# Four attentions in one kernel: the second score tile of a step is issued and read behind the step's piece instead of beside the first tile

## The chip, the cores and the metric

The kernel runs on one core of a Trainium2 chip. The metric is the device time of the whole program in microseconds (us); lower is better. The core's engines run side by side and meet only through semaphores: PE (the matrix engine, TensorE), DVE (VectorE), ACT (ScalarE), POOL (GpSimd) and SP, whose queue issues the DMAs.

## The reference

Four transformer layers on `x` of shape 4 x 512 x 256, each an attention of 16 heads of 16 dims and a feed-forward part, both with a layer norm in front and a residual sum behind:

```
x = x + _L0_attn_ref(_layernorm(x), ...)   # distances, window mask of 64, 8 key heads
x = x + _L0_ffn_ref(...)
x = x + _L1_attn_ref(_layernorm(x), ...)   # causal
x = x + _L1_ffn_ref(...)
x = x + _L2_attn_ref(_layernorm(x), ...)   # causal, rotary
x = x + _L2_ffn_ref(...)
x = x + _L3_attn_ref(_layernorm(x), ...)   # no mask
x = x + _L3_ffn_ref(...)
...
attn = softmax(q @ k.T * scale + mask)     # per head, 512 x 512
out  = attn @ v
```

## The kernel before

The first attention (called a0 here) is `attention_window`, the other three (a1, a2, a3) are `attention_quads`; a1 and a2 are causal, a3 has no mask. The change touches the loop of these two functions and nothing else.

**Two kinds of scores.** The softmax is taken over keys, and the kernel wants the exponentials with keys on the partitions, so that they can be multiplied with V without a transpose. So it computes the scores twice. First `scores(t)` makes a tile with 128 queries on the partitions (up to 512 keys in the columns, fewer in the causal attentions), and DVE reads it only for the row maxima: `maxima(t)` (`minima(t)` in a0), L1165 and L440. Below such a tile is called s. When the 16 tiles of a group of four heads are read, POOL splits the maxima into two numbers (`split_maxima`), PE turns them, and ACT and DVE write them into rows of q, so that the second product has the maximum subtracted. Then `scores_T(N)` makes the transposed scores of two heads (two matmuls, called T below), ACT takes their exponential, and `values(J)` multiplies two steps' exponentials with V (called V).

**Two halves of the array.** A head's q and k take 64 partitions: head a = 0 the partitions 0 to 63, head a = 1 the partitions 64 to 127. Matmuls of T and s therefore use 64 of PE's 128 rows ("64*128" in the profile's rows), those of V and of the pieces use all. s tiles alternate: tile 2N + 24 has a = 0 and PSUM bank 4, tile 2N + 25 has a = 1 and bank 5. Below s0 and s1 are these two tiles of step N. A tile may be written only when the tile before it in its bank is read (`pe.wait_ge(max_done, t - 1)`).

**Steps and pieces.** A batch and attention has 32 steps, there are four batches, so 128 steps N per attention. The s tiles run 24 tiles (LEAD) ahead of T. A table `plan` puts at most one piece into each step: all the rest of the attention cut up, each piece using PSUM bank 7: `turn` and `project` make the next batch's q and k, `values` its V, `maxima` the turn of the maxima, `group` the turn of a finished group (DVE then divides, `finish_group`), `heads` and `outputs` the output product. Before it writes bank 7, PE waits until the piece before is taken out of it (`freed`).

PE's program order in a step is T, s0, s1, V (in odd steps), piece. DVE's is maxima of s0, maxima of s1, its share of the piece, then an `exchange` (rotary) or layer norm work of a later batch in a few steps. ACT's is the exponential and its share of the piece. In the causal attentions every s and T is followed by two short matmuls that add the mask in the same half and bank (L1423, L1425 and L1447, L1451); in a0 T is (L708).

Of the kernel before, what the change touches and what calls it, by code (L numbers as in the profile page):

```python
# [14 lines left out]
NB = 4  # L15
# [144 lines left out]
def attention_window(nc, tag, X, cst, PS, scr, filled, weights, rope, scale, dist, slopes, masks, preset_m, bias):  # L160
# [8 lines left out]
    TILES_ = 2 * STEPS  # L169
    LEAD = 24  # L170
# [5 lines left out]
    with ExitStack() as ctx:  # L176
# [101 lines left out]
        with nc.Block() as block:  # L278
# [137 lines left out]
            def _(dve):  # L416
# [99 lines left out]
                sigmoid(1)  # L516
                keep_minima(0, 0)
                for N in range(FULL):
                    for t in (2 * N + LEAD, 2 * N + LEAD + 1):
                        if t < NB * TILES_:  # L520
                            minima(t)
                    piece(*piece_at(N))
                    if N % STEPS in swaps and N // STEPS + 1 < NB:
                        exchange(N // STEPS + 1, swaps[N % STEPS])
                    c = N // STEPS + 2
                    if c < NB:
                        if N % STEPS == 23:
                            layer_norm_stats(dve, ln, c, source(c))
                        elif N % STEPS == 25:
                            dve.wait_ge(transposed, 2 * KC * c)  # L530
                            layer_norm_apply(dve, ln, c, source(c))
                        elif N % STEPS == 26:
                            total(c)
                        elif N % STEPS == 28:
                            sigmoid(c)
                for x in LAST:
                    piece(*x)

# [102 lines left out]
            def _(pe):  # L641
# [155 lines left out]
                pe.wait_ge(masks_done, 2)  # L797
                for N in range(FULL):
                    scores_T(N)
                    for t in (2 * N + LEAD, 2 * N + LEAD + 1):  # L800
                        if t < NB * TILES_:
                            scores(t)
                    if N % 2 and N >= 3:
                        values((N - 3) // 2)
                    piece(*piece_at(N), previous_piece(N))
                values(FULL // 2 - 1)
                before = previous_piece(FULL)
                for x in LAST:
# [6 lines left out]
def attention_quads(nc, tag, X, Y, cst, PS, scr, filled, weights, spans, masks=None, rope=None, bias=None,  # L815
# [13 lines left out]
    LEAD = 24  # L829
    FULL = NB * STEPS  # L830
    SCALE = HD ** -0.5
    with ExitStack() as ctx:
# [319 lines left out]
        def vector_program(dve):  # L1152
            p = Names()

            def source(c):
                return lambda t: X[:, TB * c + t, :]
# [91 lines left out]

            def loop():
                for N in range(FULL):  # L1250
                    for t in (2 * N + LEAD, 2 * N + LEAD + 1):
                        if t < NB * TILES_:
                            maxima(t)
                    piece(*piece_at(N))
                    if N % STEPS in swaps and N // STEPS + 1 < NB:
                        exchange(N // STEPS + 1, swaps[N % STEPS])
                    if N % STEPS == 24 and N // STEPS + 2 < NB:
                        layer_norm_stats(dve, ln, N // STEPS + 2, source(N // STEPS + 2))
                    if N % STEPS == 26 and N // STEPS + 2 < NB:
                        dve.wait_ge(transposed, KC * (N // STEPS + 2))  # L1260
                        layer_norm_apply(dve, ln, N // STEPS + 2, source(N // STEPS + 2))
                for last in LAST:
                    piece(*last)

# [112 lines left out]
        def tensor_program(pe):  # L1377
# [164 lines left out]
            def loop():  # L1542
                for N in range(FULL):
                    scores_T(N)
                    for t in (2 * N + LEAD, 2 * N + LEAD + 1):
                        if t < NB * TILES_:
                            scores(t)
                    if N % 2 and N >= 3:
                        values((N - 3) // 2)
                    piece(*piece_at(N), previous_piece(N))  # L1550
                values(FULL // 2 - 1)
                before = previous_piece(FULL)
                for last in LAST:
# [1777 lines left out]
```

## Time and profile before

| | |
|---|---|
| device time, median of 3 runs | 1834.86 us (1834.26 to 1839.75) |
| the profiled execution's own time | 1827.52 us |
| its span, first to last instruction | 1825.7 us |
| busy share of the span | PE 88%, PE's weight loads 53%, DVE 62%, ACT 48%, POOL 26% |
| loops of the attentions, from the span's start | a0 about 70 to 336 us, a1 532 to 767, a2 914 to 1148, a3 1420 to 1673 |

The profile is one execution. It rests on the start and end of every instruction; for PE the ends are modelled, so a busy PE is not a PE at its peak, and two matmuls in different halves of the array count as one busy stretch. Weight loads (PEld) are rows of their own. In a row of a timeline the first number is the start in us from the span's start, the second the length in us, and the bracket behind it tells how long the engine sat idle before it and what ended that.

### The profile page before, as it was taken

To read this page: it belongs to the slowest core of one execution; us is meant where nothing else is said; L and a number is where in the kernel's file an instruction comes from. 1 tells how busy PE (TensorE), PEld (TensorE's weight loads), DVE (VectorE), ACT (ScalarE), POOL (GpSimd) and SP (SyncE) were. 2 spreads that over 40 slices of the span, in tenths; PEclk is the share of its full clock that TensorE was granted. 3 is DMA by queue.
4 is the path that set the end of the run, shared out by engine and by line. 5 is a ranking of instruction groups with operands and counts; after the bars stand their busy time and mean duration, and the time that the engine had idled before them with its cause. 6 is when DMAs were issued, how large, how long until landed. Compare 5 with 4: busy or idle time off the path is not lost. (4 is left out here: it accounts for less than half of the span.)

```text
span 1825.7 us, 28978 instructions
## 1 busy us (share of the span) xinstructions
PE 1608.8 (88%) x10726; PEld 963.0 (53%) x10726; DVE 1134.3 (62%) x2567; ACT 867.9 (48%) x1361; POOL 469.0 (26%) x596
## 2 busy tenths in 40 slices
PE   5899999799989999952999999689999999998776
PEld 2344444388866666541556665367764444443533
DVE  2787787333446666468577776355545788774475
ACT  1256565533325555532155555457761666665322
POOL 4222210033322330010333220036762522300000
PEclk9999999999989999965999999879999999999698
DMA  7452350200235424000643560211206435320322
GB/s 248 107 128 65 81 145 1 95 0 0 77 91 162 133 80 114 1 10 27 178 116 83 128 162 2 87 45 54 80 25 174 112 80 145 115 48 13 112 94 93
DMA packets 68962, 160.30 MB, mean 88 GB/s; under 512 B 10286, under 2 KB 15927, under 8 KB 67963
## 3 DMA queue, kind: packets, MB, share of 16 engines
q1 hardware_dynamic: 68826, 158.51, 30.6%
q8 instruction: 83, 1.36, 0.3%
q14 instruction: 53, 0.43, 0.1%
HBM read 109.05 MB, written 53.09 MB: 89 GB/s over the span
## 5 line engine op out<-in xcount | busy, mean ns | idle before, releaser
L1165 DVE TENSOR_REDUCE a_mx<-PS 128x1 f32<-128x512 f32 (+3 forms) x768 | 392.3, 551 | 188.1 <-PE PS L1425 128.1
L1362 ACT ACTIVATE a_pT<-PS 128x1024 f32<-128x1024 f32 (+3 forms) x384 | 310.2, 811 | 228.1 <-PE PS L1451 159.2
L1420 PE MATMUL PS<-a_k,a_q 64*128 64x512 f32 (+3 forms) x768 | 233.9, 415 | 16.7 <-DVE a_mx L1165 13.6
L440 DVE CUSTOM_DVE_ANT_0 PS<-PS,a_dist 128x448 f32<-128x448 f32 x256 | 156.1, 643 | 51.1 <-PE PS L685 48.7
L1442 PE MATMUL PS<-a_q,a_k 64*128 64x512 f32 (+3 forms) x768 | 174.0, 437 | 7.2 <-PEq L98 2.0
L1465 PE MATMUL PS<-a_pT,a_va 128*32 128x512 f32 (+3 forms) x1536 | 164.5, 500 | 3.1 <-ACT a_raw L1315 2.9
L590 ACT ACTIVATE a_pT<-PS 128x448 f32<-128x448 f32 (+1 forms) x256 | 124.6, 541 | 84.6 <-PE PS L708 84.2
L1442 PEld LDWEIGHTS PS<-a_q,a_k 64*128 64x128 f32 x768 | 76.0, 185 | 144.9 <-issue 70.5
L1420 PEld LDWEIGHTS PS<-a_k,a_q 64*128 64x128 f32 x768 | 109.0, 187 | 69.9 <-DVE a_mx L1165 57.0
L157 PE MATMUL PS<-cst 128*128 128x512 f32 x192 | 102.9, 667 | 36.7 <-PEq L98 28.6
L2361 POOL TENSOR_TENSOR f_h_low<-f_prod,f_h_high 128x512 fp32r<-128x512 f32 x84 | 109.9, 1315 | 60.4 <-ACT f_h_high L2548 57.6
L1423 PE MATMUL PS<-a_half_masks 64*128 64x128 bf16 x512 | 100.6, 229 | 0.0
L2484 DVE TENSOR_TENSOR f_prod<-PS,f_gb 128x512 f32<-128x512 f32 x84 | 57.3, 688 | 67.8 <-ACT PS L2574 65.9
L685 PE MATMUL PS<-a_k,a_q 64*128 64x448 f32 x256 | 86.1, 461 | 12.1 <-DVE a_mx L440 5.5
L1290 ACT ACTIVATE a_q<-PS 16x1024 fp32r<-16x1024 f32 x48 | 48.7, 1014 | 79.2 <-PE PS L1473 78.8
L1425 PE MATMUL PS<-a_half_masks 64*128 64x64 bf16 x512 | 86.3, 190 | 0.0
L2574 ACT ACTIVATE PS<-PS,f_b 128x512 f32<-128x512 f32 x84 | 55.4, 660 | 50.2 <-PE PS L2648 50.0
L157 PEld LDWEIGHTS PS<-cst 128*128 128x128 f32 x192 | 36.2, 207 | 75.7 <-issue 68.4
L1102 POOL TENSOR_TENSOR a_mxh<-a_mx,a_m 128x16 fp32r<-128x16 f32 x48 | 10.8, 225 | 239.2 <-DVE a_mx L1165 239.2
L721 PE MATMUL PS<-a_pT,a_va 128*32 128x512 f32 x512 | 68.2, 604 | 1.6 <-ACT a_raw L598 1.1
L1710 POOL TENSOR_TENSOR f_h_low<-f_hid,f_h_high 128x512 fp32r<-128x512 f32 x32 | 41.2, 1292 | 94.3 <-ACT f_h_high L1809 94.3
L1170 DVE TENSOR_SCALAR a_q<-PS 16x1024 fp32r<-16x1024 f32 x48 | 59.0, 1230 | 7.3 <-PE PS L1473 5.7
(362 smaller groups left out, 3436.6 us busy)
## 6 DMA issues: line engine op xcount, KB each, us to landing
spread_scratch<-a_high SPq DMA_DIRECT2D x96, 256.0 KB, 3.0
a_q<-spread_scratch SPq DMA_DIRECT2D x96, 256.0 KB, 5.5
a_k<-spread_scratch SPq DMA_DIRECT2D x96, 256.0 KB, 6.2
f_gb<-gate_rows SPq DMA_DIRECT2D x68, 256.0 KB, 5.2
spread_scratch<-a_low SPq DMA_DIRECT2D x48, 256.0 KB, 4.0
a_q<-window_scratch SPq DMA_DIRECT2D x32, 256.0 KB, 5.6
a_k<-window_scratch SPq DMA_DIRECT2D x32, 256.0 KB, 6.4
window_scratch<-a_high SPq DMA_DIRECT2D x24, 256.0 KB, 4.7
```

Of the source, the lines that this page charges most:

```text
L157: pe.matmul(PS[:, bank, :], cst[:, C_ID:C_ID + P], cst[:, 0:512], start=True, stop=True)
L440: dve.tensor_tensor_reduce(PS[:, 4 + a, 0:KW], PS[:, 4 + a, 0:KW], dt_[:, off:off + KW], 1.0, 3e38, ALU.add, ALU.min, mx[:, gg % 2, qt, 2 ...
L590: act.activation(pT[rows, buffer_of(kt), 2 * half + a, GLOB:S], PS[rows, 2 * half + a, GLOB:S], ACT.Exp, scale=-float(slopes[2 * pair + a] ...
L685: pe.matmul(PS[:, 4 + a, 0:KW], q[rows, b % 2, pair, qt * P:(qt + 1) * P], k[rows, b % 2, pair, GLOB:S], start=True, stop=True).then_inc(s ...
L1165: dve.tensor_reduce(mx[:, gg % 2, qt, 2 * half + a:2 * half + a + 1], PS[:, tile_bank(t), 0:kw], AX.X, ALU.max).then_inc(max_done, 1)
L1362: act.activation(pT[:, N // 2 % 2, N % 2, :, q0:S], PS[:, 2 * (N % 2):2 * (N % 2) + 2, q0:S], ACT.Exp, scale=SCALE).then_inc(exp_done, 1)
L1420: mm = pe.matmul(ps[:, 0:kw], q[b % 2][rows, pair, qt * P:(qt + 1) * P], k[b % 2][rows, pair, 0:kw], start=True, stop=not causal)
L1423: pe.matmul(ps[:, kw - P:kw], half_masks[rows, 0, 0, :], half_masks[rows, 1, 0, :], start=False, stop=False)
L1425: mm = pe.matmul(ps[:, kw - 64:kw], half_masks[rows, 0, 1, :], half_masks[rows, 1, 1, 64:P], start=False, stop=True)
L1442: mm = pe.matmul(PS[:, 2 * half + a, q0:S], k[b % 2][rows, pair, kt * P:(kt + 1) * P], q[b % 2][rows, pair, q0:S], start=True, stop=not ca ...
L1465: mm = pe.matmul(PS[BLK * i:BLK * i + BLK, 6, q0:S], va[b % 2][:, kt, GH * g + i, :], pT[:, J % 2, i // 2, i % 2, q0:S], start=(kt == 0), ...
L2361: pool.tensor_tensor(h_low[:, G % 6, :], prod[:, G % 6, :], h_high[:, G % 6, :].bitcast(F32), ALU.subtract).then_inc(h_low_done, 1)
```

## The change

In all four attentions the second s tile of each step moves to the step's end. On PE the order becomes T, s0, V (in odd steps), piece, s1. On DVE it becomes maxima of s0, exchange or layer norm work, the piece, maxima of s1. No instruction is added, removed or resized; ACT, POOL and SP keep their order. The tiles' banks and waits stay: s1 still waits for the maxima of the s1 before.

```diff
@@ DVE, attention_quads (attention_window alike)
                 for N in range(FULL):
-                    for t in (2 * N + LEAD, 2 * N + LEAD + 1):
-                        if t < NB * TILES_:
-                            maxima(t)
-                    piece(*piece_at(N))
+                    if 2 * N + LEAD < NB * TILES_:
+                        maxima(2 * N + LEAD)
                     if N % STEPS in swaps and N // STEPS + 1 < NB:
                         exchange(N // STEPS + 1, swaps[N % STEPS])
...
                         layer_norm_apply(dve, ln, N // STEPS + 2, source(N // STEPS + 2))
+                    piece(*piece_at(N))
+                    if 2 * N + LEAD + 1 < NB * TILES_:
+                        maxima(2 * N + LEAD + 1)
@@ PE, both functions
                     scores_T(N)
-                    for t in (2 * N + LEAD, 2 * N + LEAD + 1):
-                        if t < NB * TILES_:
-                            scores(t)
+                    if 2 * N + LEAD < NB * TILES_:
+                        scores(2 * N + LEAD)
                     if N % 2 and N >= 3:
                         values((N - 3) // 2)
                     piece(*piece_at(N), previous_piece(N))
+                    if 2 * N + LEAD + 1 < NB * TILES_:
+                        scores(2 * N + LEAD + 1)
```

PE in a3, a stretch of three steps (from 1506.59 us of the trace). L1442 are the two T, L1420 the s tiles, L1479 the piece that turns a finished group, L1465 V, L1473 the piece that turns the maxima. Before:

```order
L1442 MATMUL PS<-a_q_17470,a_k_17471 128x512 x2
L1420 MATMUL PS<-a_k_17471,a_q_17470 128x512 x2
L1479 MATMUL PS<-cst,a_raw 128x128 x4
L1442 MATMUL PS<-a_q_17470,a_k_17471 128x512 x2
L1420 MATMUL PS<-a_k_17471,a_q_17470 128x512 x2
L1465 MATMUL PS<-a_pT,a_va_17476 32x512 x4
L1442 MATMUL PS<-a_q_17470,a_k_17471 128x512 x2
L1420 MATMUL PS<-a_k_17471,a_q_17470 128x512 x2
L1473 MATMUL PS<-cst,a_m 128x128 x4
```

The same steps after the change (T is now L1445, s L1423, V L1468, the pieces L1482 and L1476):

```order
L1445 MATMUL PS<-a_q_17470,a_k_17471 128x512 x2
L1423 MATMUL PS<-a_k_17471,a_q_17470 128x512
L1482 MATMUL PS<-cst,a_raw 128x128 x4
L1423 MATMUL PS<-a_k_17471,a_q_17470 128x512
L1445 MATMUL PS<-a_q_17470,a_k_17471 128x512 x2
L1423 MATMUL PS<-a_k_17471,a_q_17470 128x512
L1468 MATMUL PS<-a_pT,a_va_17476 32x512 x4
L1423 MATMUL PS<-a_k_17471,a_q_17470 128x512
L1445 MATMUL PS<-a_q_17470,a_k_17471 128x512 x2
L1423 MATMUL PS<-a_k_17471,a_q_17470 128x512
L1476 MATMUL PS<-cst,a_m 128x128 x4
```

Each T now stands between two single s tiles: s1 of the step before, in the upper half, ahead of it, and its own s0, in the lower half, behind it.

DVE in a1, the place in the second batch where layer norm statistics of a later batch (L126 to L130) meet the piece `outputs` (L1204, after the change L1206). Before:

```order
L1204 TENSOR_TENSOR X<-X,PS 128x512
L126 BN_STATS a_ln_stats<-X 128x6 x4
L128 MEMSET a_ln_held 128x1
L130 BN_AGGR a_ln_meanvar<-a_ln_stats 128x2 x4
L1165 TENSOR_REDUCE a_mx<-PS 128x1 x4
```

After:

```order
L126 BN_STATS a_ln_stats<-X 128x6 x4
L128 MEMSET a_ln_held 128x1
L130 BN_AGGR a_ln_meanvar<-a_ln_stats 128x2 x4
L1206 TENSOR_TENSOR X<-X,PS 128x512
L1167 TENSOR_REDUCE a_mx<-PS 128x1 x4
```

The piece's read of bank 7 now stands behind the statistics; the place is there once in a1 and once in a2.

## Rows read from the trace of the kernel before

**Rows 1.** The page: span, and busy us, share of the span, instructions by engine.

```profile
span 1825.7 us, 28978 instructions
PE 1608.8 (88%) x10726; PEld 963.0 (53%) x10726; DVE 1134.3 (62%) x2567; ACT 867.9 (48%) x1361; POOL 469.0 (26%) x596
```

**Rows 2.** Windows over the loops of a0 and a3: length, each engine's busy us, PE's clock, DMA.

```profile
80.00:345.00 265.00, 252.61 (x1752) 116.45 (x1751) 196.81 (x570) 159.32 (x311) 47.22 (x83) 1.00 0.29 75
...
1420.00:1680.00 260.00, 249.26 (x1381) 112.30 (x1380) 191.10 (x319) 168.41 (x191) 60.74 (x90) 1.00 0.32 86
```

**Rows 3.** Waits, whole span: who waited for whom, us in total, times, longest.

```profile
PEld PS L1420 <- DVE a_mx L1165: 57.0, 120, 1.8
PEld PS L685 <- DVE a_mx L440: 34.3, 82, 1.1
```

**Rows 4.** Timeline of a3, PE, its weight loads and DVE, 1504.9 to 1509.2.

```profile
1504.93 0.51 PE L1442 MATMUL PS<-a_q,a_k 64*128 64x512 f32 x2
...
1505.59 1.07 PE L1465 MATMUL PS<-a_pT,a_va 128*32 128x512 f32 x8
...
1506.59 0.49 PE L1442 MATMUL PS<-a_q,a_k 64*128 64x512 f32 x2
1506.92 0.61 PE L1420 MATMUL PS<-a_k,a_q 64*128 64x512 f32 x2
1507.04 0.18 PEld L1420 LDWEIGHTS PS<-a_k,a_q 64*128 64x128 f32 x1 [0.15 <-DVE a_mx L1165]
...
1507.42 1.29 DVE L1165 TENSOR_REDUCE a_mx<-PS 128x1 f32<-128x512 f32 x2 [0.44 <-PE PS L1420]
...
1507.46 0.65 PE L1479 MATMUL PS<-cst,a_raw 128*128 128x128 f32 x4
1508.04 0.50 PE L1442 MATMUL PS<-a_q,a_k 64*128 64x512 f32 x2
...
1508.38 0.87 PE L1420 MATMUL PS<-a_k,a_q 64*128 64x512 f32 x2
...
1508.63 0.25 DVE L1178 RECIPROCAL a_rs<-PS 128x16 f32<-128x16 f32 x1
1508.76 0.18 PEld L1420 LDWEIGHTS PS<-a_k,a_q 64*128 64x128 f32 x1 [0.41 <-DVE a_mx L1165]
...
1508.91 0.42 DVE L1181 TENSOR_TENSOR a_at<-PS,a_rs 128x256 f32<-128x256 f32 x1
1509.18 1.07 PE L1465 MATMUL PS<-a_pT,a_va 128*32 128x512 f32 x8
```

**Rows 5.** Timeline of a1, PE: two steps with nothing between them.

```profile
580.49 0.38 PE L1420 MATMUL PS<-a_k,a_q 64*128 64x256 f32 x1
580.50 0.49 PE L1442 MATMUL PS<-a_q,a_k 64*128 64x512 f32 x1
...
580.81 0.47 PE L1442 MATMUL PS<-a_q,a_k 64*128 64x512 f32 x1
...
580.88 0.22 PE L1451 MATMUL PS<-a_half_masks 64*128 64x128 bf16 x1
...
581.13 0.20 PE L1447 MATMUL PS<-a_half_masks 64*128 64x64 bf16 x1
```

**Rows 6.** Timeline of a1, PE: s tiles of 512 and 128 columns.

```profile
563.00 0.48 PE L1420 MATMUL PS<-a_k,a_q 64*128 64x512 f32 x2
563.15 0.23 PE L1423 MATMUL PS<-a_half_masks 64*128 64x128 bf16 x1
...
563.33 0.23 PE L1423 MATMUL PS<-a_half_masks 64*128 64x128 bf16 x1
```

**Rows 7.** Timeline of a1, DVE: statistics behind the piece `outputs`.

```profile
643.52 0.69 DVE L1204 TENSOR_TENSOR X<-X,PS 128x512 f32<-128x512 f32 x1 [1.49 <-PE PS L1501]
644.12 1.40 DVE L126 BATCH_NORM_STATS2 a_ln_stats<-X 128x6 f32<-128x256 f32 x4
...
645.86 0.85 DVE L1165 TENSOR_REDUCE a_mx<-PS 128x1 f32<-128x256 f32 x2
```

More of the change, by code:

```diff
@@ L518, in _ @@
                 for N in range(FULL):
-                    for t in (2 * N + LEAD, 2 * N + LEAD + 1):
-                        if t < NB * TILES_:
-                            minima(t)
-                    piece(*piece_at(N))
+                    if 2 * N + LEAD < NB * TILES_:
+                        minima(2 * N + LEAD)
                     if N % STEPS in swaps and N // STEPS + 1 < NB:
@@ L535, in _ @@
                             sigmoid(c)
+                    piece(*piece_at(N))
+                    if 2 * N + LEAD + 1 < NB * TILES_:
+                        minima(2 * N + LEAD + 1)
                 for x in LAST:
@@ L1250, in loop @@
                 for N in range(FULL):
-                    for t in (2 * N + LEAD, 2 * N + LEAD + 1):
-                        if t < NB * TILES_:
-                            maxima(t)
-                    piece(*piece_at(N))
+                    if 2 * N + LEAD < NB * TILES_:
+                        maxima(2 * N + LEAD)
                     if N % STEPS in swaps and N // STEPS + 1 < NB:
@@ L1261, in loop @@
                         layer_norm_apply(dve, ln, N // STEPS + 2, source(N // STEPS + 2))
+                    piece(*piece_at(N))
+                    if 2 * N + LEAD + 1 < NB * TILES_:
+                        maxima(2 * N + LEAD + 1)
                 for last in LAST:
@@ L1544, in loop @@
                     scores_T(N)
-                    for t in (2 * N + LEAD, 2 * N + LEAD + 1):
-                        if t < NB * TILES_:
-                            scores(t)
+                    if 2 * N + LEAD < NB * TILES_:
+                        scores(2 * N + LEAD)
                     if N % 2 and N >= 3:
@@ L1550, in loop @@
                     piece(*piece_at(N), previous_piece(N))
+                    if 2 * N + LEAD + 1 < NB * TILES_:
+                        scores(2 * N + LEAD + 1)
                 values(FULL // 2 - 1)
```

## The prediction

> **What bounds the kernel now.** I read the page first: PE is busy for 88% of the span, no other engine for more than 62% [rows 1]. Then the windows over the attention loops, which make some 990 us of the span (the four lengths in the table): PE is busy for nearly all of each, at its full clock (1.00, the 2.4 GHz level), and DVE for 197 of 265 us in a0 and 191 of 260 in a3 [rows 2]. So in the loops PE is the engine that the time follows, and whatever holds PE there is paid in full. The list of waits names one holder above all: a weight load of an s tile that stood until DVE had read the tile before it in the same bank, 57.0 us in 120 waits in a1 to a3 and 34.3 us in 82 in a0 [rows 3].
>
> The timeline of a3 shows how that looks [rows 4]. T of 1504.93 and its two s tiles are over at 1505.59, when V starts: 0.66 us for T, s0 and s1, both pairs side by side in the two halves. At 1506.92 s0 starts, but the load of s1 stands for 0.15 us and ends up at 1507.04; the stretch takes 0.87 us (1506.59 to 1507.46). In the next step s0 starts at 1508.38, s1 only at 1508.76, after 0.41 us of standing, and the stretch takes 1.14 us. The reason is that DVE gets s0 and s1 at once and reads them one behind the other, 1.29 us for two (1507.42 to 1508.71), while the step's PE work is short, and its piece (0.25 and 0.42 us) comes on top. The lower half of the array is idle all the while, since V and the pieces need both halves.
>
> **The change part by part.**
>
> *Work.* No instruction is added, so the sum has only waits and the packing of the two halves.
>
> *Packing.* s1 no longer runs beside s0. It stands behind the piece and ahead of the next T, whose first matmul is in the other half. What that gives is in the trace, where two steps of a1 follow each other with nothing between [rows 5]: s1 starts at 580.49, the next T's lower matmul at 580.50, 0.01 us later, and T's upper one at 580.81, when the upper half is free. The mask matmul L1451 of the lower half starts at 580.88, before one that stands ahead of it in the program, L1447 of the upper half (581.13). So each half takes its own work in its own order. After the change the lower half has T and s0, the upper one s1 and T: as much as before, and the switches between half and whole array are as many. I cost the packing at nothing. If the halves had to keep the program's common order, the price would be about 0.31 us a step (580.50 to 580.81) in the three attentions with masks behind T; that is a rival below.
>
> The Trainium skill speaks against this reading: "TensorE: Matmul & The Clock Gate", Part 3, says that matmuls start and end strictly in program order and that only weight loads are pulled ahead. By that rule the masks and s0 would stand behind T's upper matmul. The rows differ from the rule, so the sum goes by the rows.
>
> *Balance in a1 and a2.* There s0 and s1 have different widths, and the wide one changes halves from step to step. Before, narrow and wide run side by side and the stretch lasts as long as the wide one: both start at 563.00, the masks of the 128-column tile at 563.15, those of the 512-column one at 563.33 [rows 6], so a narrow tile in a stretch saves 0.18 us. After, a stretch holds s1 of the step before and its own s0: by the program's table of tiles these are the two narrow ones in odd steps and the two wide ones in even steps. 64 odd steps in each of two attentions, half with 128 against 512 columns (0.18 us), half with 256 against 384, a third of that difference in columns (0.06 us): 128 x 0.12 = 15 us if PE never stood. Other waits will eat some; I take 8, between 0 and 15.
>
> *Holds.* The 202 held loads stand for 91.3 us [rows 3]. Each also loses the cover of its weight load: a held s1 needs 0.42 us to the next whole-array matmul (1508.76 to 1509.18), an unheld one 0.33 (0.66 less the 0.33 from T to s, 1506.59 to 1506.92), so 0.09 x 202 = 18 us more. The pool is 109 us. How much of it goes I work out in the worst place, the two steps behind 1506.59. Call T's start 0. A stretch is 0.66, the piece 0.58 (1507.46 to 1508.04), V 1.00 (1505.59 to 1506.59), a tile comes to DVE 0.5 us after its start (1506.92 to 1507.42) and takes 0.65 there. DVE reads the s1 of before from 0.5 to 1.15, s0 to 1.8, does the piece to 2.45, reads s1 (started at 1.24) to 3.1 and the next s0 to 3.75. PE wants the next s0 at 1.57 and gets its bank at 1.8: held 0.23. It wants the next s1 at 3.13, bank free at 3.1: not held. The s0 after that, wanted at 3.46, is held 0.29. Before, this place has 0.21 and 0.48 over the 0.66 and the holds go on; so about half stays there. Where the hold is only 0.15 or so, it goes entirely, because s1's bank now has a whole step without s0's read just ahead of it. Such heavy places (behind `group` and `maxima`) make some three quarters of the pool. 0.75 x 0.5 + 0.25 = 0.6 of 109 is 65 us. Bounds: 0 (DVE's work per step is the same) and all 109.
>
> *What is late now.* T's upper matmul starts one s tile later, about 0.31 us, so the exponential too. The next user of it comes two steps later, and ACT is busy for 168 of 260 us in a3 [rows 2]; I take 3 us in all. On DVE the statistics (644.12 to 645.86, 1.7 us) move ahead of the 0.69 us of `outputs` [rows 7], whose bank the next step's piece waits for; behind that piece on PE now stands s1. That is one place in a1 and one in a2: at most 1.7 us each, I take 2 for both. On POOL the maxima's split waits one piece and V longer for the last s1 of a group; the turn of the maxima is two steps later, so that is hidden; uncovered it would cost at most those 1.6 us (1.00 and 0.58) in each of 64 groups.
>
> *Sum.* -65 - 8 + 3 + 2 = -68 us, all in the four loops. The profiled execution's own time is 1827.5 us, 1.8 over its span and 7.3 under the median of the three runs; the saving is the same on both: 1759 for a profiled execution, **1767 us** for the median. DVE would then be busy for 191 of some 243 us in a3, 79%, which leaves it room.
>
> **The rivals.**
>
> *A. The holds come back.* DVE has the same two tiles and the same piece to do in each step, each bank is still refilled once a step, and s1's read now queues behind a piece that itself waits for PE. For it: half of the holds stay in the walk above. Against it: most holds have DVE idle just before (0.44 us at 1507.42) while PE did V, so the loss is in the bunching and not in DVE's load. With a tenth to a third of the pool gone the time is 1798 to 1824, at worst 1835, no change. Chance 0.18, half of it within 0.3%.
>
> *B. The halves don't pass each other (slower).* If with s1 in front the lower half's masks and s0 wait for T's upper matmul, each of 384 steps in a0, a1 and a2 loses 0.31 us, 119 us; less the 65 of the holds and without the balance it ends near 1835 + 119 - 65 + 5 = 1894. It decides where more than about half of the steps lose it. Against it: rows 5 show the passing in just this arrangement [rows 5]. The skill's rule on program order ("TensorE: Matmul & The Clock Gate", Part 3) would give this case. Chance 0.08.
>
> *C. Nearly all holds go.* -109 - 15 + 5, near 1716. It needs DVE to keep up at the heavy places too. Chance 0.04.
>
> **How the numbers follow.** My forecast has 0.70 and by itself runs from 1742 to 1795 (0.35 to 0.8 of the pool). The range of 1738 to 1826 leaves out C, B and the upper end of A, together a little under 0.2. 0.3% is 5.5 us, about what a measurement of this kernel tells from no change. Faster: 0.70 + 0.04 + half of A, 0.83. Same: 0.09. Slower: 0.08.
>
> **What would show it.** Right: the two rows of PE's weight loads waiting for DVE's maxima fall from 91.3 us to some 35; a3's loop shortens by about 18 us, a0's by 20 or more, a1's and a2's by about 15 each; in a timeline s1 starts within 0.01 us of the next T's lower matmul. Rival A: the same rows stay near 90, now also on s0. Rival B: in each half the masks start only when T's upper matmul is done, and the loops grow in a0 to a2 but not in a3. The feed-forward parts should keep their times. The prediction is wrong if the piece is now what PE waits with: then waits for bank 7 and for the exponential would have grown.

## The result and the profile after

The changed kernel takes 1809.29 us (median of 4 runs, 1806.98 to 1815.86) against 1834.57 for the kernel before on the same chip: a ratio of 0.986, 95% interval 0.983 to 0.989, some 25 us faster. The profiled execution's own time is 1807.41 us, 20 under the one of before. The forecast was 1767. One run of all those below was disturbed, a run of `before_short` that took 6927.49 us; it is left out of that kernel's time and ratio.

The page after and the windows over a0 and a3 (columns as in [rows 1, 2]):

```profile
span 1805.5 us, 28972 instructions
PE 1564.8 (87%) x10720; PEld 963.8 (53%) x10726; DVE 1133.3 (63%) x2567; ACT 874.4 (48%) x1361; POOL 470.4 (26%) x596
...
80.00:345.00 265.00, 249.57 (x1771) 127.28 (x1768) 202.41 (x584) 159.53 (x312) 47.75 (x87) 0.99 0.29 77
1400.00:1660.00 260.00, 246.25 (x1403) 113.56 (x1402) 199.76 (x336) 172.09 (x191) 69.45 (x104) 1.00 0.35 93
```

These windows now reach further past the ends of the loops. From the first T to the last, PE is busy for 246.9 of 257.5 us in a0 (255.9 of 265.5 before) and for 231.7 of 243.0 in a3 (243.3 of 252.6 before), DVE for 203.7 and 188.6 us (202.1 and 189.1 before), and PE's mean clock is the same in both kernels (0.99 and 1.00). The list of waits answers to [rows 3]; the last row is the one of the kernel before that belongs to the third:

```profile
PEld PS L1423 <- DVE a_mx L1167: 168.8, 299, 1.8
PEld PS L686 <- DVE a_mx L440: 62.7, 85, 1.4
PE PS L1423 <- DVE a_mx L1167: 40.0, 79, 1.4
...
PE PS L1420 <- DVE a_mx L1165: 13.6, 27, 1.4
```

The two rows that were to fall from 91.3 to 35 us rose to 231.5. That is not the loss it looks like: s1's load now queues behind V or the piece and stands while these matmuls keep PE busy. The standing of PE itself, with both halves idle, is in a row of its own: 40.0 us, against 13.6 before. Neither row is the price of the holds: a held s1 beside a running s0 costs time too, and there PE counts as busy.

The loops, from the start of the first T to the start of the last T, in us, of each kernel's profiled execution (so are all loop lengths below):

| kernel | a0 | a1 | a2 | a3 | sum |
|---|---|---|---|---|---|
| before | 265.5 | 234.8 | 233.4 | 252.6 | 986.3 |
| changed | 257.5 | 231.7 | 232.9 | 243.0 | 965.1 |

So all of the gain of these two executions, 21 us, is in the loops, almost half of it in a3. The timeline of a3 from behind `group` to `maxima`, PE, its loads of s and DVE, shows what became of the holds of [rows 4]:

```profile
1464.73 0.50 PE L1423 MATMUL PS<-a_k,a_q 64*128 64x512 f32 x1
1464.73 0.73 PE L1445 MATMUL PS<-a_q,a_k 64*128 64x512 f32 x2
1465.16 0.25 DVE L1180 RECIPROCAL a_rs<-PS 128x16 f32<-128x16 f32 x1
1465.30 0.18 PEld L1423 LDWEIGHTS PS<-a_k,a_q 64*128 64x128 f32 x1 [0.28 <-DVE a_mx L1167]
...
1465.44 0.42 DVE L1183 TENSOR_TENSOR a_at<-PS,a_rs 128x256 f32<-128x256 f32 x1
1465.73 1.07 PE L1468 MATMUL PS<-a_pT,a_va 128*32 128x512 f32 x8
...
1466.73 0.18 PEld L1423 LDWEIGHTS PS<-a_k,a_q 64*128 64x128 f32 x1 [0.84 <-DVE a_mx L1167]
...
1467.55 0.66 PE L1476 MATMUL PS<-cst,a_m 128*128 128x128 f32 x4
```

s1 and T start together (1464.73). Now s0 stands (0.28 us, with `finish_group` still in front of DVE's next reads), and the stretch takes 1.00 us (1464.73 to 1465.73) where an unheld one takes 0.66; the next takes 0.82 (1466.73 to 1467.55). Over 0.66 that is 0.34 and 0.16; my walk had 0.23 and 0.29 for these two steps. Before, the same two steps of this batch had 0.47 (a stretch of 1.13 us) and 0.15 (0.81 us); the 0.21 and 0.48 of [rows 4] are the step ahead of `group` and the one behind it. The step ahead of this `group` fell from 0.89 to 0.71 us, the one behind `maxima` from 1.13 to 0.90. And 0.84 us of standing at 1466.73 cost PE nothing: V was running.

A new place is the head of a stretch. In a1, behind the piece `maxima`:

```profile
542.11 1.23 DVE L1172 TENSOR_SCALAR a_q<-PS 16x1024 fp32r<-16x1024 f32 x1
...
542.49 0.64 PE L1468 MATMUL PS<-a_pT,a_va 128*32 128x256 f32 x8
...
543.37 0.49 DVE L1167 TENSOR_REDUCE a_mx<-PS 128x1 f32<-128x128 f32 x2
543.72 0.50 PE L1423 MATMUL PS<-a_k,a_q 64*128 64x512 f32 x1 [0.59 <-DVE a_mx L1167]
```

DVE copies the turned maxima into q (1.23 us), then reads the tile queued behind. The next s1 waits for that, T stands behind s1 in PE's queue (it starts at 543.83), and PE does nothing for 0.59 us.

### The profile page after: what moved, and what is told of

Its sections match the earlier page's. It is cut to its first block and busy times, and to the rows that moved or that the text cites. A ratio compares the mean times of both kernels' runs of the same rounds, so it can differ in the third digit from the quotient of the medians.

```text
span 1805.5 us, 28972 instructions
## 1 busy us (share of the span) xinstructions
PE 1564.8 (87%) x10720; PEld 963.8 (53%) x10726; DVE 1133.3 (63%) x2567; ACT 874.4 (48%) x1361; POOL 470.4 (26%) x596
## 5 line engine op out<-in xcount | busy, mean ns | idle before, releaser
L1423 PE MATMUL PS<-a_k,a_q 64*128 64x512 f32 (+3 forms) x768 | 303.0, 432 | 40.9 <-DVE a_mx L1167 40.0
L1445 PE MATMUL PS<-a_q,a_k 64*128 64x512 f32 (+3 forms) x768 | 263.5, 417 | 3.4 <-PEq L98 2.0
L1423 PEld LDWEIGHTS PS<-a_k,a_q 64*128 64x128 f32 x768 | 134.4, 185 | 208.6 <-DVE a_mx L1167 168.8
L1468 PE MATMUL PS<-a_pT,a_va 128*32 128x512 f32 (+3 forms) x1536 | 164.6, 500 | 5.5 <-ACT a_raw L1318 5.1
L1445 PEld LDWEIGHTS PS<-a_q,a_k 64*128 64x128 f32 x768 | 126.4, 186 | 14.9 <-issue 8.4
L686 PE MATMUL PS<-a_k,a_q 64*128 64x448 f32 x256 | 114.5, 468 | 12.2 <-DVE a_mx L440 8.5
L1426 PE MATMUL PS<-a_half_masks 64*128 64x128 bf16 x512 | 115.4, 229 | 0.0
L1454 PE MATMUL PS<-a_half_masks 64*128 64x128 bf16 x512 | 107.3, 220 | 0.0
L1450 PE MATMUL PS<-a_half_masks 64*128 64x64 bf16 x512 | 98.4, 201 | 0.0
L1428 PE MATMUL PS<-a_half_masks 64*128 64x64 bf16 x512 | 96.4, 190 | 0.0
L686 PEld LDWEIGHTS PS<-a_k,a_q 64*128 64x128 f32 x256 | 46.5, 186 | 82.0 <-DVE a_mx L440 62.7
L701 PE MATMUL PS<-a_q,a_k 64*128 64x448 f32 (+1 forms) x256 | 82.5, 414 | 2.4 <-DVE a_q L446 2.4
```

What stands on the lines that cost most here:

```text
L686: pe.matmul(PS[:, 4 + a, 0:KW], q[rows, b % 2, pair, qt * P:(qt + 1) * P], k[rows, b % 2, pair, GLOB:S], start=True, stop=True).then_inc(s ...
L1423: mm = pe.matmul(ps[:, 0:kw], q[b % 2][rows, pair, qt * P:(qt + 1) * P], k[b % 2][rows, pair, 0:kw], start=True, stop=not causal)
L1426: pe.matmul(ps[:, kw - P:kw], half_masks[rows, 0, 0, :], half_masks[rows, 1, 0, :], start=False, stop=False)
L1445: mm = pe.matmul(PS[:, 2 * half + a, q0:S], k[b % 2][rows, pair, kt * P:(kt + 1) * P], q[b % 2][rows, pair, q0:S], start=True, stop=not ca ...
L1454: mm = pe.matmul(PS[:, 2 * half + a, q0:q0 + P], half_masks[rows, 0, 1, :], half_masks[rows, 2, 1, :], start=False, stop=True)
L1468: mm = pe.matmul(PS[BLK * i:BLK * i + BLK, 6, q0:S], va[b % 2][:, kt, GH * g + i, :], pT[:, J % 2, i // 2, i % 2, q0:S], start=(kt == 0), ...
```

## Experiments

Three groups: how large is the pool of holds and what does the packing cost by itself; what does DVE's order cost; can the new stalls be taken out. Each time is the median; each ratio is to the kernel before on the same chip, with its 95% interval.

Loop lengths are of one execution each, and one thing in them doesn't come from the edit: for some us PE is granted the lower clock level (1.2 GHz), mostly at the start of a loop, and not for equally long in every execution. `free_after` and `free_inter`, two kernels explained below, have the same instructions in a0. Windows from 69 to 76 us, the first of `free_after`:

```profile
69.00:76.00 7.00, 7.00 (x33) 4.46 (x34) 1.61 (x10) 4.03 (x8) 3.00 (x4) 0.59 0.00 0
...
69.00:76.00 7.00, 6.38 (x47) 3.84 (x48) 2.66 (x13) 3.92 (x8) 3.46 (x4) 1.00 0.00 0
```

At a clock of 0.59 PE does 33 matmuls in the 7 us, at 1.00 it does 47, and the whole loop takes 244.3 us against 241.5. So here is also the difference of two kernels' loops, step by step from T's start to the next T's start, over those steps alone in which both traces have PE at the full clock (109 to 127 of 127 steps), in us:

| difference | a0 | a1 | a2 | a3 | sum |
|---|---|---|---|---|---|
| changed less before | -8.0 | -1.3 | -0.8 | -9.6 | -19.7 |
| `after_short` less `before_short` | 7.2 | 6.7 | 7.9 | 2.1 | 23.9 |
| `free_after` less `free_before` | 7.2 | 2.0 | 3.2 | 1.6 | 14.0 |
| `before_short` less `free_before` | 0.7 | 1.5 | 1.6 | -0.9 | 2.9 |
| `after_short` less `free_after` | 0.8 | 6.2 | 6.3 | -0.4 | 12.9 |
| `free_inter` less `free_after` | 0.0 | -3.3 | -2.5 | 0.0 | -5.8 |
| `free_inter_a0` less `free_after` | -1.5 | -0.1 | 0.0 | 0.0 | -1.6 |
| `interleaved` less changed | 0.0 | -0.1 | -0.1 | 0.1 | -0.1 |
| `inter_a0` less changed | -2.2 | -0.1 | 0.0 | -0.1 | -2.4 |
| `late_s1` less changed | 0.9 | -1.3 | -1.3 | 0.2 | -1.5 |
| `both` less changed | -0.8 | -1.0 | -1.3 | 0.2 | -2.9 |
| `before_keep` less before | 0.1 | -7.1 | -7.0 | -6.5 | -20.5 |
| `after_keep` less changed | 0.0 | -9.5 | -9.5 | -7.6 | -26.6 |
| `ln_last` less changed | 2.2 | 1.1 | 4.9 | 3.3 | 11.5 |
| `piece_v` less changed | 4.4 | 1.9 | 2.7 | 2.5 | 11.5 |
| `pe_only` less changed | 12.8 | 3.1 | 9.9 | 17.0 | 42.8 |
| `shifted` less before | -0.8 | 3.0 | 1.9 | -1.5 | 2.6 |

Loops that an edit doesn't touch agree within 0.1 us. Below, "at the full clock" means this table.

### The pool, and the packing with the holds gone

`before_short` and `after_short` are the kernels before and changed with

```diff
-dve.tensor_reduce(mx[...], PS[:, tile_bank(t), 0:kw], AX.X, ALU.max)
+dve.tensor_reduce(mx[...], PS[:, tile_bank(t), 0:kw:8], AX.X, ALU.max)
```

and the same step of 8 in a0's `tensor_tensor_reduce`.

> The kernel before, but DVE's maxima (and a0's minima) read every eighth column of a score tile only, in all four attentions; so a part of each row's maximum is left out. A read then ends in some 0.15 to 0.25 us and no s tile should stand for the one before it. It measures the pool of holds by itself. My pool of 109 us (91.3 of standing, 18 of lost cover): 1835 - 109 = about 1726, range 1710 to 1750. If less than 60 us go, the stretches have another limit than DVE's reads, and the pool was counted too high.

> The changed kernel with the same short reads (every eighth column), a part of each row's maximum left out in the same way. Theory H (the change only moves the holds from s1 onto s0 and onto s1 at the head of the next stretch; the packing of the halves costs nothing): within 10 us of the kernel before with short reads, or up to 15 faster for the balance of widths. Theory P (s1 ahead of T couples the halves or adds a switch, a cost that holds have nothing to do with): slower than the kernel before with short reads by 20 to 40 us, in a0 to a2 above all. The gap between the changed kernel and this one measures the holds that are left in it: 80 to 100 us by H, under 60 by P.

Measured: 1719.38 us, ratio 0.939 (0.934 to 0.945), and 1746.19 us, 0.952 (0.947 to 0.957). The rows of their loads' waits for DVE, first of `before_short`:

```profile
PEld PS L1420 <- DVE a_mx L1165: 18.2, 28, 1.4
```

then of `after_short`:

```profile
PEld PS L1423 <- DVE a_mx L1167: 115.6, 195, 1.4
```

The pool was sized right: 0.061 x 1835 is 111 us (I had 109). But the changed order is some 25 us slower once the reads are short (27 by the times, 24 at the full clock), as theory P said. The gap from the changed kernel to `after_short` is 54 us in the loops (965.1 to 911.2) and 63 by the ratios, nearer P's "under 60" than H's 80 to 100. In `before_short` T's loads wait for the exponential, 64.9 us in 95 waits; whether that costs PE anything isn't shown, since PE itself has no such wait in that trace.

`free_before` and `free_after` have the short reads and a short copy of the turned maxima as well:

```diff
-dve.tensor_scalar(q[b % 2][96:112, 2 * g:2 * g + 2, :], PS[96:112, 7, :]...
+dve.tensor_scalar(q[b % 2][96:112, 2 * g:2 * g + 2, 0:64], PS[96:112, 7, 0:64]...
```

> The kernel before with DVE nearly free: it reads every eighth column of an s tile (part of each row's maximum is left out) and its share of the piece maxima copies 64 of 512 columns (the rest of the turned maxima is left out), in all four attentions. Nothing should hold an s tile. It is the base for the two runs below; about 1705 to 1720, a0 234 to 238, a1 and a2 210 to 214, a3 217 to 220.

> The changed kernel with the same two parts left out. With no holds left the gap to the kernel above is the packing alone. Theory C (s0 and T's mask start only when T's upper matmul, queued behind s1, has been started; this bites where the two halves' work has unequal lengths): a0 longer by 5 to 7 us (some 25 stretches with T of 64 columns of output, 1.15 instead of 0.91 us), a1 and a2 by 2 to 4 us each (coupling 4 to 5 less the balance), a3 by 0 to 2: 10 to 17 us in all. Theory N (the packing costs nothing; the 26 us between the two kernels with short reads were holds behind DVE's pieces): under 4 us in all.

Measured: 1713.30 us, ratio 0.932 (0.929 to 0.936), and 1730.61 us, 0.943 (0.940 to 0.946). The loops part the costs:

| kernel | a0 | a1 | a2 | a3 | sum |
|---|---|---|---|---|---|
| before_short | 237.9 | 213.0 | 213.9 | 220.0 | 884.8 |
| after_short | 245.1 | 222.2 | 221.8 | 222.1 | 911.2 |
| free_before | 237.2 | 214.5 | 212.3 | 220.9 | 884.9 |
| free_after | 244.3 | 216.3 | 215.5 | 222.5 | 898.6 |

With DVE free the changed order costs 13.7 us (898.6 less 884.9): a0 7.1, a1 1.8, a2 3.2, a3 1.6 (at the full clock 14.0). That is the packing. The other 12.6 us between `after_short` and `free_after`, nearly all in a1 and a2, are stalls behind the 1.23 us copy. In the order of before the copy costs 2.9 us at the full clock once the reads are short; the sums of the table don't show it, because `free_before` has about 10 us of the lower clock in a1 and `before_short` none. And from `free_before` and `free_after` the holds of the full kernels follow: 986.3 - 884.9 = 101.4 us before, 965.1 - 898.6 = 66.5 after. They fell by 35.

In a0, the packing shows where T has only 64 columns of output. `after_short`, PE and its loads:

```profile
131.86 0.47 PE L686 MATMUL PS<-a_k,a_q 64*128 64x448 f32 x1
...
131.87 0.66 PE L701 MATMUL PS<-a_q,a_k 64*64 64x448 f32 x2
...
132.46 0.11 PEld L709 LDWEIGHTS PS<-a_near,a_eye 64*64 64x64 bf16 x2 [0.35 <-issue]
...
132.62 0.47 PE L686 MATMUL PS<-a_k,a_q 64*128 64x448 f32 x1
...
133.02 0.66 PE L730 MATMUL PS<-cst,a_m 128*128 128x128 f32 x4
```

and `before_short`:

```profile
128.96 0.41 PE L700 MATMUL PS<-a_q,a_k 64*64 64x448 f32 x2
129.31 0.10 PEld L708 LDWEIGHTS PS<-a_near,a_eye 64*64 64x64 bf16 x2 [0.21 <-issue]
...
129.47 0.47 PE L685 MATMUL PS<-a_k,a_q 64*128 64x448 f32 x2
...
129.87 0.20 PEld L729 LDWEIGHTS PS<-cst,a_m 128*128 128x128 f32 x2 [0.22 <-issue]
```

1.16 us against 0.91: mask and s0 of the lower half start 0.25 us later, although their own half is free. There are 28 such places, and the two steps of every eight that have such a T make up 6.7 of the packing's 7.2 us in a0 (`free_after` less `free_before`).

### The order of issue within a stretch

In a1 the same coupling stands behind wide s tiles. PE of the changed kernel:

```profile
583.70 0.50 PE L1423 MATMUL PS<-a_k,a_q 64*128 64x512 f32 x1
583.71 0.32 PE L1445 MATMUL PS<-a_q,a_k 64*128 64x128 f32 x1
583.88 0.20 PE L1450 MATMUL PS<-a_half_masks 64*128 64x64 bf16 x1
584.04 0.23 PE L1426 MATMUL PS<-a_half_masks 64*128 64x128 bf16 x1
584.05 0.23 PE L1454 MATMUL PS<-a_half_masks 64*128 64x128 bf16 x1
...
584.12 0.49 PE L1423 MATMUL PS<-a_k,a_q 64*128 64x512 f32 x1
584.14 0.30 PE L1445 MATMUL PS<-a_q,a_k 64*128 64x128 f32 x1
...
584.64 0.66 PE L1476 MATMUL PS<-cst,a_m 128*128 128x128 f32 x4
```

The lower half's first mask (583.88) starts ahead of T's upper matmul (584.14), which stands before it in the program, as in [rows 5]. But its second mask (584.05) starts only with the upper half's first (584.04), and s0 0.42 us after the stretch's start. `interleaved` issues the lower half's work first where s1 is wider than T (the first `...` stands for the two mask matmuls of this half):

```diff
 for a in range(2):
     mm = pe.matmul(PS[:, 2 * half + a, q0:S], k..., q...)   # T, cut short
+    if between is not None:                            # s1 wider than T
...
+        if a == 0:
+            scores(between)                            # s0
...
-    if 2 * N + LEAD < NB * TILES_:
+    if 2 * N + LEAD < NB * TILES_ and not wide_before(N):
         scores(2 * N + LEAD)
```

> The changed kernel, but in a1 and a2, where s1 is wider than T, PE's order is: s1, T of the lower half with its masks, s0 with its masks, T of the upper half with its masks. Theory C (s0 doesn't start before T's upper matmul, which stands ahead of it in the program and waits for s1; that eats the gain from the equal widths): the stretches of T 128 with two s of 512 fall from 0.94 to about 0.75 us, those of T 256 with 384 and 512 from 0.88 to about 0.80, 4 to 5 us in each of a1 and a2, 8 to 10 in all. Rival (the stretch is limited by something else, or a held s0 now holds the upper T as well): 0 or up to 5 us slower, the stretches as before or longer.

`free_inter` is that order with DVE free:

> The same, DVE nearly free with the same parts left out, on the changed kernel with s0 ahead of T's upper matmul where s1 is wider than T (a1 and a2 only). By theory C the wide stretches fall (0.94 to 0.77, 0.88 to 0.81 us) and nothing takes it back, so a1 and a2 are 4 to 5 us shorter than in the run above, each, and a little shorter than in the kernel before with free DVE: the balance of widths that I had counted. If they stay within 1 us, the order of issue within a stretch is not what costs.

Measured: `free_inter` 1719.21 us, ratio 0.937 (0.934 to 0.940), a1 213.0 and a2 213.0: 5.8 us under `free_after`, and together 0.8 under `free_before`. The order of issue was the cost in a1 and a2, as theory C says, though it gives back 3.3 and 2.5 us and not 4 to 5 in each. `interleaved` 1816.55 us, 0.992 (0.989 to 0.995), not faster than the changed kernel. Its loops are 234.7 us (a1) and 232.9 (a2); a1 is 3.0 us longer than the changed kernel's, but PE was at the lower clock for about 7 us more in it, and at the full clock the two kernels are 0.1 us apart in each loop. Its timeline, PE, loads of s and DVE, shows why `interleaved` gains nothing:

```profile
553.90 0.50 PE L1423 MATMUL PS<-a_k,a_q 64*128 64x512 f32 x1
...
554.15 0.47 PE L1423 MATMUL PS<-a_k,a_q 64*128 64x512 f32 x1
...
554.53 1.29 DVE L1167 TENSOR_REDUCE a_mx<-PS 128x1 f32<-128x512 f32 x2 [0.81 <-PE PS L1428]
554.67 0.66 PE L1488 MATMUL PS<-cst,a_m 128*128 128x128 f32 x4
...
555.28 0.32 PE L1423 MATMUL PS<-a_k,a_q 64*128 64x128 f32 x1
...
555.88 0.18 PEld L1423 LDWEIGHTS PS<-a_k,a_q 64*128 64x128 f32 x1
...
556.23 0.42 PE L1480 MATMUL PS<-a_pT,a_va 128*32 128x256 f32 x4
```

s0 now starts 0.25 us after s1, and the stretch takes 0.77 us instead of 0.94. But the two tiles reach DVE together, the next s0 stands until 555.88 and its stretch takes 0.95 (555.28 to 556.23) instead of 0.81. From this wide stretch to T behind DVE's copy of the maxima it is 3.56 us (553.90 to 557.46), and 3.57 at such a place in the changed kernel (540.15 to 543.72).

The same order in a0, for T of 64 columns, with DVE free and on the full changed kernel:

> The changed kernel with DVE nearly free (it reads every eighth column of an s tile and copies 64 of 512 columns of its share of the turned maxima; the rest of both is left out), and in a0, in the steps whose T has 64 columns of output, PE's order s1, T of the lower half with its mask, s0, T of the upper half with its mask. Theory C (a0's 7 us are lost because s0 and the lower mask wait for T's upper matmul, which waits for s1): the 25 or so stretches of 1.15 us fall to 0.9, a0 6 us shorter than in the run with free DVE on the changed kernel (244.3), that is 238 to 239. Rival (T with 64 columns of output can't run beside s1, whatever the order): a0 stays above 243.

> The same order of issue in a0 with nothing left out. If the reads of DVE have slack there, a0 is 4 to 6 us shorter than in the changed kernel (257.5). If DVE's reads pace these places, as the changed order in a1 and a2 showed (0.94 to 0.77 us in wide stretches, but 0.81 to 0.95 in the narrow ones behind them), the holds take it back: a0 within 2 us of 257.5.

Measured: 1725.26 us, ratio 0.943 (0.939 to 0.946), a0 240.0; and 1814.26 us, 0.990 (0.987 to 0.993), a0 257.7. The 240.0 looks like 4.3 of the 7.1 us given back, but 2.8 of these are the clock of the windows above: at the full clock 1.5 us come back. With DVE's real reads it is 2.2 us, hidden in the 257.7 by about 5 us more of the lower clock. So in a0 theory C is mostly refuted, and the rival, that such a T can't run beside s1 in either order, mostly holds: on the clock of `free_after` a0 is 244.3 less 1.5, 242.8 us, where C had 238 to 239 and the rival more than 243. PE of `free_inter_a0` shows why:

```profile
173.29 0.46 PE L686 MATMUL PS<-a_k,a_q 64*128 64x448 f32 x1
173.30 0.41 PE L710 MATMUL PS<-a_q,a_k 64*64 64x448 f32 x1
...
173.84 0.46 PE L686 MATMUL PS<-a_k,a_q 64*128 64x448 f32 x1
173.85 0.41 PE L710 MATMUL PS<-a_q,a_k 64*64 64x448 f32 x1
...
174.40 0.44 PE L739 MATMUL PS<-cst,a_m 128*128 128x128 f32 x2
```

s0 now starts 0.55 us after s1 and not 0.76. But T's upper matmul (173.85), which in `free_after` starts 0.30 us after s1 and stands ahead of s0 in the program, now starts only with s0. The loss has changed halves, and the stretch takes 1.11 us where it took 1.16 and the order of before takes 0.91.

### DVE's order and its copy

`pe_only` keeps PE's new order and gives DVE its old one (s0, s1, piece):

```diff
+for t in (2 * N + LEAD, 2 * N + LEAD + 1):
+    if t < NB * TILES_:
+        maxima(t)
+piece(*piece_at(N))
-if 2 * N + LEAD < NB * TILES_:
-    maxima(2 * N + LEAD)
...
-piece(*piece_at(N))
-if 2 * N + LEAD + 1 < NB * TILES_:
-    maxima(2 * N + LEAD + 1)
```

> PE's order as changed (T, s0, V, piece, s1), DVE's order as before (maxima of s0, of s1, then the exchange or layer norm work and the piece). Theory H1 (what spoils the change is that s1's read stands behind the piece on DVE, and so s1 of the next step is held at the head of a stretch, some 21 us in all): faster than the changed kernel by 10 to 20 us, near 1792. Rival H2 (DVE then waits for s1, which PE starts only behind its piece, before it takes the piece out of bank 7; PE's next piece, the split of the maxima and the exponentials come late): slower than the changed kernel by 10 us or more, and waits for DVE's piece (keep, finish, outputs) appear on PE's next piece and on T.

Measured: 1861.84 us, ratio 1.016 (1.011 to 1.021): 53 us behind the changed kernel, H2. Its timeline in a3:

```profile
1469.79 0.65 PE L1474 MATMUL PS<-cst,a_m 128*128 128x128 f32 x4
...
1470.91 0.69 DVE L1166 TENSOR_REDUCE a_mx<-PS 128x1 f32<-128x512 f32 x1 [0.22 <-PE PS L1421]
...
1471.63 1.23 DVE L1171 TENSOR_SCALAR a_q<-PS 16x1024 fp32r<-16x1024 f32 x1
...
1472.89 1.97 DVE L1166 TENSOR_REDUCE a_mx<-PS 128x1 f32<-128x512 f32 x3
1472.96 0.50 PE L1443 MATMUL PS<-a_q,a_k 64*128 64x512 f32 x2 [0.30 <-issue]
```

DVE sits in front of an s1 that PE issues behind the piece, so the copy starts 1.84 us after the turn does, T, which needs the copied maxima, starts only behind it (1472.96), and three reads of 1.97 us pile up behind. With s1 last on PE, DVE's piece must stand ahead of its read.

`after_keep` and `before_keep` shorten the copy alone, in a1 to a3 (the diff of the free kernels):

> The changed kernel, but DVE's share of the piece maxima in a1, a2 and a3 (the copy of the turned maxima into q, 1.23 us, ahead of s1's read) writes 64 of its 512 columns; so that part of the maxima is left out for the other columns. Theory K (part of the gain was lost because this copy stands ahead of s1's read and so holds the next s1, which then holds both halves): about 48 copies of 1.23 us become about 0.2; the holds at the head of a stretch fall from 14 us in a1 to a3 to about 3, in V's 1.23 us (256 columns) to 0.70, and a1, a2 and a3 get shorter by 8 to 15 us each, 25 to 40 in all. Rival (the copy is not what DVE is late with): under 10 us in all. a0, whose copy is as it was, keeps its time.

> The kernel before with the same short copy (64 of 512 columns), the same part left out. By theory K the copy costs less here, since both tiles are read ahead of it: a1 to a3 shorter by 10 to 20 us in all, that is 10 to 20 less than what the changed kernel gains from it. Rival: as much as in the changed kernel, then the copy is a load on DVE in both orders and the order around it costs nothing.

Measured: 1782.89 us, ratio 0.972 (0.969 to 0.975), and 1804.69 us, 0.985 (0.982 to 0.988). Loops a1 to a3 shorter by 26.5 us (707.6 to 681.1) in the changed order and by 24.9 (720.8 to 695.9) in the old one. Of the 24.9 some 4 are the clock, of which the kernel before had about 10 us more at the lower level in a1 than `before_keep`; at the full clock it is 26.6 us in the changed order and 20.6 in the old one. So the truth lies between K, which had 10 to 20 us of difference, and its rival, which had none: the change didn't reach this part of the pool, some fifth of it, and made it 6 us dearer. The ratios (25 and 28 us, each with an interval of 5 us or more to either side) can't tell the two orders apart.

`ln_last` puts the layer norm and exchange work behind s1's read, `piece_v` puts the piece ahead of V on PE:

```diff
@@ ln_last, DVE
 maxima(2 * N + LEAD)
+piece(*piece_at(N))
+maxima(2 * N + LEAD + 1)
 exchange(N // STEPS + 1, swaps[N % STEPS])
 layer_norm_stats(dve, ln, N // STEPS + 2, source(N // STEPS + 2))
...
-piece(*piece_at(N))
-maxima(2 * N + LEAD + 1)
@@ piece_v, PE
+piece(*piece_at(N), previous_piece(N))
 if N % 2 and N >= 3:
     values((N - 3) // 2)
-piece(*piece_at(N), previous_piece(N))
```

> The changed kernel with DVE's order s0, piece, s1, and the exchange or layer norm work last. The two places in a0 where s1 stands for 1.27 us at the head of a stretch behind the statistics go, and the piece outputs is taken out of its bank at once: 2 to 6 us shorter than the changed kernel in all, in a0 most. Rival: the same work then stands ahead of the next step's s0 and holds that: no difference (within 2 us).

> The changed kernel with the piece ahead of V on PE in odd steps; nothing left out. If what remains of the holds comes from DVE getting its piece late (s1's read stands behind it), DVE now gets the odd steps' pieces 1.0 us earlier and s1's read finds it free: 5 to 15 us faster than the changed kernel. Rival: the pieces that matter (maxima, group) are in even steps, where nothing changes, and PE waits more for bank 7, whose piece before was taken out later than V would have covered: no change or up to 15 us slower.

Measured: 1831.12 us, ratio 0.999 (0.997 to 1.002), and 1821.82 us, 0.993 (0.990 to 0.995). Both are slower than the changed kernel. At the full clock each loses 11.5 us to it in the loops, `ln_last` most in a2 (4.9), `piece_v` most in a0 (4.4). `piece_v` went by its rival; for `ln_last` both sides were wrong, since its rival had no difference. I didn't follow which wait grew.

### Balance, and T ahead of the held s1

> The kernel before, with the pairs of s tiles shifted by one: a step's pair is tiles 2N+23 and 2N+24 instead of 2N+24 and 2N+25, both right behind T and read together on DVE, so no s1 stands ahead of T. In a1 and a2 the two tiles of a stretch then have equal widths. Theory of the balance (my term): a1 and a2 shorter by 6 to 8 us each, a0 and a3 as before (within 2 us), total 1820 to 1828. Rival (the wide tile of a pair is not what ends a stretch, DVE's reads of the pair or the masks do): no change, 1832 to 1838; or slower, since two wide tiles at once bunch DVE's reads (up to 1845).

```diff
-for t in (2 * N + LEAD, 2 * N + LEAD + 1):
-    if t < NB * TILES_:
+for t in (2 * N + LEAD - 1, 2 * N + LEAD):
+    if LEAD <= t < NB * TILES_:
```

in PE's and DVE's loops of the kernel before. Measured: 1831.43 us, ratio 1.000 (0.998 to 1.003), a1 237.6, a2 235.1 (234.8 and 233.4 before). Equal widths side by side gave nothing: a stretch of T 128 with two s of 512 takes 0.75 us unheld as before with one, but the narrow pair behind it takes 1.22, more than the mixed pair of before (0.99), where 0.60 is possible (`after_short`).

`late_s1` and `both` (`late_s1` with `inter_a0`):

```diff
 scores_T(N)
+if N % 8 == 0 and N:
+    scores(2 * N + LEAD - 1)       # s1 of the step before
...
-if 2 * N + LEAD + 1 < NB * TILES_:
+if (N + 1) % 8 and 2 * N + LEAD + 1 < NB * TILES_:
     scores(2 * N + LEAD + 1)
```

> The changed kernel, but in every eighth step, the first of a group of heads, s1 of the step before goes behind T instead of ahead of it; nothing left out. Theory Q (T is ready there as soon as DVE's copy of the maxima is done, but stands behind s1, which is held until DVE has read the two tiles queued behind that copy): V with 256 columns to the next T falls from 1.23 to about 0.75 us in a1 and a2, a1, a2 and a3 get shorter by 3 to 6 us each, 1795 to 1805 in all. Rival D (DVE paces these places): s1 or s0 is then held inside the next stretch for as long, loops within 2 us of the changed kernel's.

> Both edits together, nothing left out. By theories C and Q 1790 to 1802. By rival D no faster than the changed kernel, within 5 us.

Measured: 1809.73 us, ratio 0.987 (0.984 to 0.990), and 1809.55 us, 0.989 (0.985 to 0.992), like the changed kernel. In `late_s1`, a3's whole-array stretches with the stall at their end fall from 133.9 to 128.9 us, and its half-array ones grow from 108.8 to 114.0. The stall moved, and the loop is 243.2 against 243.0: rival D. In a1 and a2 it is 1.3 us shorter each at the full clock, within D's 2 us and short of Q's 3 to 6. No version tried beats the changed kernel's time; the gains of 1 to 3 us at the full clock are too small for the times to show.

## Why the prediction was right or wrong

The direction and the range were right, the forecast of 1767 was not: 21 us in the loops where the sum had 68. Of the 47 us between them 17 are the packing with the small terms, 30 the holds.

- **What bounds the loops**: right. PE's holds behind DVE's reads were the thing to gain, and the pool (109 us) is there: 111 by the ratio, 101 by the loops.
- **Packing, costed at nothing**: wrong, a good third of the error. With balance, late exponentials and the statistics the sum had -8 + 3 + 2 = -3 us beside the holds; with DVE free it is +13.7. The step that failed is "So each half takes its own work in its own order", read from one place, a T of 512 columns beside an s of 256. A half does pass the other, but not far: in the wide stretches of a1 and a2 s0 starts 0.25 or 0.42 us after s1, by what stands between them in the program. The Trainium skill's rule ("TensorE: Matmul & The Clock Gate", Part 3), that matmuls start strictly in program order, is not what these rows show either (583.88 starts ahead of 584.14), but it was right as a warning. Rival B had this mechanism at 0.31 us in 384 steps; it is 0.25 us in a0 where T has 64 columns (6.7 us in all) and 0.17 us in a wide stretch of a1 or a2.
- **Balance, 8 us**: not there as a gain. With the coupling taken out and DVE free, a1 and a2 are 0.8 us under `free_before`: at the full clock the odd steps, with the narrow pair, gain 9.3 us, about what I had, but the even ones, with the wide pair, lose 8.8, and I had priced these at nothing. Narrow stretches do get to 0.60 us in the free kernel, yet in the full one DVE still reads the two wide tiles of the stretch before (0.81). I priced a narrow stretch by PE alone.
- **Holds, 0.6 of the pool**: 35 of 101 us went, a third: the larger part of the error. The walk behind `group` met its sum (0.52 us over 0.66 in two steps, measured 0.50), partly by luck, since its parts, 0.23 and 0.29, were 0.34 and 0.16. Reading "about half stays" off it was wrong. I set its 0.52 against the 0.21 and 0.48 of one step earlier, and even of these 0.52 is three quarters; of the 0.62 that the same two steps had before, four fifths stayed. Extending it was wrong too: I gave every heavy place a DVE piece of 0.65 us, but the copy of the maxima takes 1.23 and stands ahead of s1's read, and its cost rose from some 20 to some 26 us. "Where the hold is only 0.15 or so, it goes entirely" is not what happened: the hold of 0.15 ahead of `maxima` is there as before (0.81 and 0.82 us), while the 0.23 ahead of `group` fell to 0.05.
- **The layer norm statistics**: I looked for their price at bank 7. It is at s1: in a0, two places like 125.02 where PE stands 1.20 us behind them. Moving them (`ln_last`) costs more than they do in these two places.
- **What would show it**: a3's loop lost 9.6 us, not 18, a0's 8.0, not 20, a1's 3.1 and a2's 0.5, not 15 each. The row of waits that I named as the witness misled, since a load that stands behind a running V costs nothing.

Rival A, the holds come back, has the band (1798 to 1824) and most of the mechanism. Open: which of DVE's operations holds each part of the 66.5 us that are left; and why in a0 neither order lets the halves pass, 5.6 of its 7.1 us of packing.

## What to carry to other kernels

Where two engines pass single tiles back and forth through two banks, moving one tile in the order mostly moves the stall: price a new order over a whole period, with every consumer operation at its own length (the rare 1.23 us copy, not the usual 0.65), and first time the kernel with the consumer's work made short, before and after: that gives the pool and the cost of the new order apart. The standing of loads is no price: with 91.3 us of it the holds cost 101 us, with 231.5 they cost 66.5. And before a difference of a few us between two loops is laid to an edit, compare their clocks: 2.8 of the 4.3 us of `free_inter_a0` were the clock.

## What the runs showed of the hardware

Two halves of the array run apart only over a short distance of the program: the lower half's first mask passed T's upper matmul by 0.26 us, its second waited for the upper half's own mask (584.05 behind 584.04), and ordering the lower half's work first cut the stretch from 0.94 to 0.77 us. With a T of 64 columns the same order only changed which half waits: T's upper matmul then started with s0, 0.56 us after s1 (173.85 behind 173.29), and the stretch fell from 1.16 to 1.11 us, not to 0.91. DVE's read of an s tile has a floor. Groups by line, the changed kernel (busy us, mean ns):

```profile
L1167 DVE TENSOR_REDUCE a_mx<-PS 128x1 f32<-128x512 f32 x384 | 250.1, 686 | 95.0 <-PE PS L1428 50.6 <-PE PS L1423 43.3
```

and `after_short`:

```profile
L1167 DVE TENSOR_REDUCE a_mx<-PS 128x1 f32<-128x64 f32 x384 | 81.5, 223 | 186.9 <-PE PS L1423 107.9 <-PE PS L1428 73.1
```

An eighth of the columns, read in steps of 8, takes a third of the time (223 against 686 ns), and 16 columns, the shortest read of `after_short`, still take 167 ns.
